# An iterated entmax stage: result matmuls taken apart by head, Newton steps spread one by one, three of eight relu pairs on ScalarE

## The chip, the cores and the metric

The kernel runs on one core of one Trainium2 chip. The metric is the time of one execution in microseconds (us), as the median of several runs on the chip: 2030.03 us for the kernel before (three runs, 2029.74 to 2032.66). Five engines work side by side and meet at semaphores: PE (TensorE, matrix products), DVE (VectorE), ACT (ScalarE), POOL (GpSimd) and SP (which issues DMAs). Each runs its own list of instructions strictly in order, so an instruction that waits holds up everything behind it on its engine.

## The reference, cut to what matters

The whole program is two residual blocks on x of 2 x 1024 x 256. The change touches one stage of the second block, a Hopfield layer (`_L1_attn_ref`): eight heads, a memory of 256 patterns, three steps of entmax with exponent 1.5, and an output projection.

```python
def entmax15(x):
    x = (x - jnp.max(x, -1, keepdims=True)) / 2.0
    ...
    return jnp.square(jnp.clip(x - tau_star, 0.0, None))
Q = layernorm(hidden, g_state, b_state) @ Wq.T
K, V = ...                               # of the normed memory, by head
xi = Q.reshape(B, S, H, hd).transpose(0, 2, 1, 3)
for _ in range(NUM_STEPS):               # 3
    scores = jnp.einsum('bhsd,hnd->bhsn', xi, K) * beta
    w = entmax15(scores)
    xi = jnp.einsum('bhsn,hnd->bhsd', w, V)
out = xi.transpose(0, 2, 1, 3).reshape(B, S, H * hd) @ Wo.T
```

tau_star is the threshold at which the squares of the clipped values sum to one. The kernel doesn't sort: it starts from a bound out of the eight largest scores and corrects the threshold in three rounds of a Newton-like step that needs the mean and the variance of the clipped scores.

## The kernel before, in words

The rows of x are 16 tiles of 128 rows. Two tiles make a chain; four chains make a group, and there are two groups. A work item g (0 to 23) is one of the three steps of one chain: items 0 to 3 are the first steps of group one, 4 to 7 their second steps, 8 to 11 their last, and 12 to 23 the same for group two. An item holds 16 score matrices (2 tiles x 8 heads) of 128 x 256, in the tile `sw[g % 5]`; two heads of one tile are a pair `q`, so an item has eight pairs.

The stage is a pipeline of 28 beats, written out by hand for each engine. In beat b:

- PE multiplies item b's scores in four quarters (`scores`, L1412, into `pss`), and turns (transposes) the squared weights of item b-3 pair by pair (`turn`, L1397, into the ring of two tiles `pt`). Where an item ends its chain (`ends`), its result is multiplied with the folded output weights (`result`, L1424, into `pz`); where a new chain begins, its normed rows are transposed (`state`, L1436, also into `pz`).
- ACT copies scores out (`sw<-pss`, L1488), makes the clipped scores of the first BY_ACT pairs of each round (`relus`, `ra`, L1468), takes the square roots (`root`, L1475), and for item b-3 cuts each pair with the final threshold (`cut`, L1495) and squares what PE has turned (`square`, `sw<-pt`, L1480). The order is cut 0, cut 1, cut 2, square 0, cut 3, square 1 and so on, with the last quarter of the scores and the root of round 1 in the middle.
- POOL makes the clipped scores of the other pairs (`most`, `rp`, L1569) behind two small instructions on `tau` and `step`, and weighs the sums of the largest (`spread`, L1577 and L1580).
- DVE finds the eight largest of each row (`largest`, L1725, 16 in a beat) and their running sums (L1599), the first threshold (`least`, L1606), the mean and variance of each clipped pair (`moments`: BATCH_NORM_STATS2, L1711 for ACT's pairs and L1715 for POOL's; 24 in a beat), and the Newton steps on 128 x 16 tiles (`newton`, L1623 to L1691). It also adds results to x (L1740) and writes the new states (`xt`, L1733).

Three items are in their rounds at once: in beat b item b-3 is in round 2, b-2 in round 1, b-1 in round 0. `newton` is a generator: each `yield` is a place where another instruction may come between two steps. `moments` calls `next` on it twice behind each of its eight instructions, and `finish` runs what is left. A round's threshold (`neg_made`) frees ACT's and POOL's clipped scores of the next round, and after round 2 ACT's cuts.

The rings that matter: `pss` and `pt` have two tiles each, `ra` seven and `rp` six, `pz` two, `sw` five items. Below, "turn phase" is the stretch of a beat in which PE's turns and ACT's cuts and squares follow each other, and "first turn" is its first turn on PE.

Of the kernel before, what the change touches and what calls it, by code (L numbers as in the profile page):

```python
# [16 lines left out]
P = 128  # L17
# [1298 lines left out]
class Hopfield(Stage):  # L1316
# [7 lines left out]
    BY_ACT = 4  # L1324
# [48 lines left out]

    def view(self, g, q):

        return self.sw[g % 5][:, q // 4, 2 * (q % 4):2 * (q % 4) + 2, :]
# [9 lines left out]
    def pe(self, e):  # L1386
# [40 lines left out]

        def state(g, i):
            n = self.tile(g, i)
            e.wait_ge(self.xn_made, n + 1)  # L1430
            if n >= 2:
                e.wait_ge(self.xt_made, n - 1)
            if self.ends(g - 6):
                e.wait_ge(self.y_out, self.tile(g - 6, i) + 1)
            for c in range(DC):
                x = e.transpose(self.pz[i][:, c * P:(c + 1) * P], self.xn[n % 2][:, c * P:(c + 1) * P], k.ident[:])  # L1436
            x.then_inc(self.state_in, 1)
# [3 lines left out]
        for beat in self.beats():  # L1441
            if beat < self.n:
                scores(beat, 0, 0)
                scores(beat, 0, 1)
            if self.begins(beat + 1):
                for i in range(2):
                    state(beat + 1, i)
            if beat < self.n:
                scores(beat, 1, 0)
                scores(beat, 1, 1)  # L1450
            for i in range(2):
                if self.ends(beat - 4):
                    result(beat - 4, i)
                if 0 <= beat - 3 < self.n:
                    for q in range(4 * i, 4 * i + 4):
                        turn(beat - 3, q)

    def act(self, e):
# [40 lines left out]
        for beat in self.beats():  # L1499
# [21 lines left out]
            if 2 in rounds:  # L1521
                root(rounds[2], 2)
# [85 lines left out]
    def newton(self, e, g, r, step, read_a, read_p):  # L1608
# [23 lines left out]
        if r == 0:  # L1632
            x.then_inc(self.asked[c], 1)
            step(e.reciprocal(rec, m))
            at = step.n
            yield
            e.wait_ge(self.root_made[c], 3 * (g // 4) + 1)
            step(e.tensor_tensor(root, z, root, ALU.subtract))
            yield
            e.wait_ge(self.math, step.n)  # L1640
# [52 lines left out]
    def dve(self, e):  # L1693
# [11 lines left out]
        def moments(g, r, between):  # L1705
            st = self.st[g % 4][r % 2]
            pool, act = range(self.BY_ACT, self.PAIRS), range(self.BY_ACT)
            for q in [*pool, *act] if r == 2 else [*act, *pool]:
# [9 lines left out]
                next(between, None)  # L1718
            finish(between)

        def largest(g, i, half):
            n = 4 * g + 2 * i + half
            e.wait_ge(self.s_made, n + 1)
            for h in range(4 * half, 4 * half + 4):
                e.max(self.top[g % 4][:, 8 * i + h, :], self.sw[g % 5][:, i, h, :]).then_inc(self.top_made, 1)  # L1725

        def state(g, i):
            n = self.tile(g, i)
            e.wait_ge(self.state_in, n + 1)
            if g >= 12:  # L1730
                e.wait_ge(self.scored, 4 * (g - 11))
            for c in range(DC):
                x = e.tensor_scalar(self.xt[g % 4][:, i, c, :], self.pz[i][:, c * P:(c + 1) * P], self.gs[:, c:c + 1],  # L1733
                                    self.bs[:, c:c + 1], ALU.mult, ALU.add)
            x.then_inc(self.xt_made, 1)
# [9 lines left out]
        for beat in self.beats():  # L1745
# [4 lines left out]
            finish(late)  # L1750
            if 1 <= beat <= self.n:
                self.least(e, beat - 1)
            if self.ends(beat - 5):
                result(beat - 5, 1)
            if w is not None:
                largest(w, 0, 0)
            after = self.newton(e, rounds[2], 2, step, self.bn_a, self.bn_p) if 2 in rounds else iter(())
            if 1 in rounds:
                moments(rounds[1], 1, after)
            finish(after)  # L1760
            if self.begins(beat + 1):
                for i in range(2):
                    state(beat + 1, i)
            if w is not None:
                largest(w, 0, 1)
            after = self.newton(e, rounds[1], 1, step, self.bn_a, self.bn_p) if 1 in rounds else iter(())
# [3 lines left out]
            if self.ends(beat - 4):  # L1770
                result(beat - 4, 0)
            late = self.newton(e, rounds[0], 0, step, self.bn_a, self.bn_p) if 0 in rounds else iter(())
            if w is not None:
                largest(w, 1, 0)
                largest(w, 1, 1)
# [793 lines left out]
```

## Time and profile before

| | us |
| --- | --- |
| median of three runs | 2030.03 |
| the profiled execution, its own time | 2029.85 |
| its span in the trace | 2028.1 |
| the Hopfield stage within it, first state to last addition | 718 to 1477 |
| mean granted TensorE clock | 0.905 of full |

| engine | busy us | share of the span |
| --- | --- | --- |
| PE | 1749.9 | 86% |
| DVE | 1545.7 | 76% |
| ACT | 1279.2 | 63% |
| POOL | 595.4 | 29% |

The shares are means over stages with different limits. In the profile's forty slices (50.7 us each) the Hopfield stage is slices 15 to 29. In most of them DVE stands at 99% and in four or five PE does; that is what has to be read by stretches. "Granted clock" is the share of its full 2.4 GHz that TensorE had in a stretch: 1.0 is all at 2.4 GHz, 0.5 all at 1.2.

### The profile page before, as it was taken

The numbers are of one execution on the slowest core, as the hardware profiler recorded it, in microseconds if no ns is written. First come the engines' busy times: TensorE is split into PE (matmuls) and PEld (weight loads), VectorE is DVE, ScalarE is ACT, GpSimd is POOL, SyncE is SP. The second block draws the span as 40 slices with busy tenths as digits, with TensorE's granted clock in tenths as the row PEclk, the third lists the DMA queues.
The fourth block names the chain that finished last, engine by engine and source line by source line (L and its number), as shares of the span: only waits on it lengthen the run. The fifth ranks groups of instructions, "written<-read, shape, count | busy, mean of one in ns | idle before, by whom it ended". The sixth has DMA issues, their size and how long they took to land. (4 is left out here: it accounts for less than half of the span.)

```text
span 2028.1 us, 32210 instructions
## 1 busy us (share of the span) xinstructions
PE 1749.9 (86%) x10498; PEld 1211.6 (60%) x10498; DVE 1545.7 (76%) x3465; ACT 1279.2 (63%) x2904; POOL 595.4 (29%) x1150
## 2 busy tenths in 40 slices
PE   4989799999998987888798988886867799998998
PEld 3558444444443775666677766665646355546787
DVE  6765889999993669999987699998266688826554
ACT  2543387777876437999875799997433288865111
POOL 2003122222222045445453344554034022224200
PEclk9989699999998987878999988888878599997999
DMA  3463132333310100000000000000025433110001
GB/s 115 134 198 63 32 64 64 64 64 65 64 33 14 58 1 1 1 0 1 1 1 1 1 1 1 1 1 1 1 75 141 89 64 64 33 56 15 1 1 42
DMA packets 36134, 82.54 MB, mean 41 GB/s; under 512 B 9600, under 2 KB 11776, under 8 KB 34944
## 3 DMA queue, kind: packets, MB, share of 16 engines
q1 hardware_dynamic: 35968, 80.48, 16.0%
q8 instruction: 85, 1.39, 0.3%
q14 instruction: 81, 0.66, 0.1%
HBM read 52.79 MB, written 27.26 MB: 39 GB/s over the span
## 5 line engine op out<-in xcount | busy, mean ns | idle before, releaser
L1035 ACT ACTIVATE probs<-pss 128x512 f32<-128x512 f32 (+3 forms) x1152 | 482.0, 496 | 132.7 <-PE pss L998 131.4
L1063 DVE TENSOR_REDUCE negmax<-px 128x2 f32<-128x1024 f32 (+2 forms) x480 | 506.7, 1113 | 51.8 <-PE px L979 48.4
L998 PE MATMUL pss<-queries,keys 64*128 64x512 f32 (+3 forms) x1152 | 296.8, 396 | 9.2 <-ACT probs L1035 5.6
L1569 POOL TENSOR_SCALAR rp<-sw,tau 128x256 f32<-128x256 f32 x576 | 274.0, 503 | 64.5 <-DVE st L1715 57.4
L979 PE MATMUL px<-keys,queries 63*128 63x512 f32 (+3 forms) x1152 | 270.1, 428 | 13.8 <-DVE negmax L1063 13.7
L1112 POOL TENSOR_SCALAR_AFFINE_SELECT probs<-probs 128x512 f32<-128x512 f32 x192 | 120.4, 635 | 532.4 <-ACT probs L1035 532.4
L998 PEld LDWEIGHTS pss<-queries,keys 64*128 64x128 f32 x1152 | 168.1, 190 | 155.8 <-ACT probs L1035 136.2
L1397 PE MATMUL pt<-ident,sw 128*128 128x128 f32 x768 | 155.6, 342 | 115.0 <-ACT sw L1480 75.3
L1012 PE MATMUL po<-probs,vals 128*32 128x512 f32 (+3 forms) x2304 | 247.3, 505 | 0.4 <-POOL probs L1112 0.2
L1468 ACT ACTIVATE ra<-sw,neg 128x256 f32<-128x256 f32 x576 | 243.3, 515 | 1.6 <-DVE neg L1691 1.6
L1412 PE MATMUL pss<-again,sw 128*128 128x256 f32 x1024 | 242.6, 401 | 0.0
L1412 PEld LDWEIGHTS pss<-again,sw 128*128 128x128 f32 x1024 | 208.1, 205 | 31.1
L1397 PEld LDWEIGHTS pt<-ident,sw 128*128 128x128 f32 x768 | 105.2, 172 | 165.4 <-ACT sw L1495 158.1
L1715 DVE BATCH_NORM_STATS2 st<-rp 128x6 f32<-128x512 f32 x288 | 194.0, 675 | 3.0 <-POOL rp L1569 3.0
L1711 DVE BATCH_NORM_STATS2 st<-ra 128x6 f32<-128x512 f32 x288 | 189.5, 679 | 7.1 <-ACT ra L1468 6.6
L1495 ACT ACTIVATE sw<-sw,neg 128x256 f32<-128x256 f32 x384 | 167.7, 497 | 19.6 <-DVE neg L1691 19.6
L979 PEld LDWEIGHTS px<-keys,queries 63*128 63x128 f32 x1152 | 132.6, 202 | 71.0 <-DVE negmax L1063 69.0
L1480 ACT ACTIVATE sw<-pt 128x512 f32<-128x512 f32 x192 | 111.1, 583 | 72.0 <-PE pt L1397 72.0
L1725 DVE MAX8 top<-sw 128x8 f32<-128x256 f32 x384 | 131.8, 410 | 10.5 <-ACT sw L1488 10.5
L1412 PE MATMUL pss<-vals,xt 128*128 128x256 f32 x512 | 119.0, 394 | 8.3 <-ACT sw L1488 8.3
L1424 PE MATMUL pz<-to_out,sw 128*128 128x256 f32 x512 | 118.4, 391 | 5.0 <-issue 4.1
L1488 ACT ACTIVATE sw<-pss 128x1024 f32<-128x1024 f32 x96 | 96.9, 1010 | 37.4 <-PE pss L1412 37.2
(355 smaller groups left out, 2591.8 us busy)
## 6 DMA issues: line engine op xcount, KB each, us to landing
queries<-rec_q SPq DMA_DIRECT2D x96, 128.0 KB, 3.5
keys<-rec_k SPq DMA_DIRECT2D x96, 128.0 KB, 3.6
queries<-rec_q SPq DMA_DIRECT2D x96, 64.0 KB, 3.4
keys<-rec_k SPq DMA_DIRECT2D x96, 64.0 KB, 3.5
rec_q<-fs SPq DMA_DIRECT2D x16, 256.0 KB, 4.4
rec_k<-fs SPq DMA_DIRECT2D x16, 256.0 KB, 4.6
rec_q<-vals SPq DMA_DIRECT2D x16, 256.0 KB
rec_k<-vals SPq DMA_DIRECT2D x16, 256.0 KB
```

Source lines behind the costliest of these rows:

```text
L979: x = e.matmul(px[:, n, s * width:(s + 1) * width], ops.qs[p][at:at + STACK, tile, t * P:(t + 1) * P], ops.ks[p][at:at + STACK, tile, c:c ...
L998: e.matmul(tl.pss[scores % 3][:, 512 - width:512], ops.ks[p][at:at + STACK + 1, tile, j * P:(j + 1) * P], ops.qs[p][at:at + STACK + 1, til ...
L1012: x = e.matmul(tl.po[32 * n:32 * n + 32, 512 - width:512], self.vals[:, u // H * QT + j, u % H, :], tl.probs[arg][:, n, :], start=j == 0, ...
L1035: e.activation(tl.probs[arg][:, w, :], tl.pss[scores % 3][:, 512 - width:512], ACT.Exp).then_inc(self.exp_made, 1)
L1063: e.tensor_reduce(out, from_px, X_AXIS, ALU.max, negate=True).then_inc(self.x_read, 1)
L1397: x = e.transpose(self.pt[n % 2][:, 2 * h + c, :], self.view(g, q)[:, h, c * P:(c + 1) * P], k.ident[:])
L1412: x = e.matmul(self.pss[n % 2][:, h, :], lhsT, rhs[:, 4 * half + h, c, :], start=c == 0, stop=c == 1)
L1468: x = e.activation(self.ra[n % 7][:, :, h], self.view(g, q)[:, h, :], ACT.Relu, bias=self.neg[c][:, 2 * q + h:2 * q + h + 1])
L1495: x = e.activation(self.view(g, q)[:, h, :], self.view(g, q)[:, h, :], ACT.Relu, bias=self.neg[c][:, 2 * q + h:2 * q + h + 1])
L1569: x = e.tensor_scalar(self.rp[rp % 6][:, :, h], self.view(g, q)[:, h, :], -BIG, self.tau[c][:, 2 * q + h:2 * q + h + 1], ALU.min, ALU.max)
L1711: e.bn_stats(st[:, q, :], self.ra[self.bn_a % 7][:].rearrange("p n h -> p (n h)")).then_inc(self.ra_read, 1)
L1715: e.bn_stats(st[:, q, :], self.rp[self.bn_p % 6][:].rearrange("p n h -> p (n h)")).then_inc(self.rp_read, 1)
```

## The change

Five edits, all in the class `Hopfield`.

1. `result` is one head instead of eight: two matmuls, with a wait for the square of that head's pair. A table `RESULTS` says per beat how many heads come before the second half of the scores, and how many behind each turn. Table `ADDS_EARLY` and `ADDS_LATE` place DVE's additions.
2. `state` transposes into `pt` instead of `pz`; the first two turns of such a beat wait until DVE has read it.
3. `BY_ACT` is 3 instead of 4: POOL makes five of eight pairs in each round.
4. Newton steps come one behind each BATCH_NORM_STATS2 (two where the pipeline runs empty), and one behind each maximum. Round 0 has eight empty places between its reciprocal and the step that waits for the root.
5. ACT takes the root of round 2 behind the second relu pair of round 0 instead of behind the last.

```diff
-    BY_ACT = 4
+    BY_ACT = 3
+    RESULTS = (((0, 0, 0) + (1,) * 8, (4,) + (1,) * 8, (4,) + (1,) * 8, (4,) + (1,) * 8, (4,) + (1,) * 8, (8,)),
+               ((0,), (16,), (16,), (16, 0, 0) + (2,) * 8))
+    ADDS_EARLY = {12: [(8, 0)], 13: [(8, 1)], 14: [(9, 0), (9, 1)], 15: [(10, 0)], 16: [(10, 1), (11, 0)], 25: [(20, 1)],
+                  26: [(21, 1)]}
+    ADDS_LATE = {16: [(11, 1)], 24: [(20, 0)], 25: [(21, 0)], 26: [(22, 0), (22, 1)], 27: [(23, 0)]}
...
 # turn(g, q)
+            if q < 2 and self.begins(g + 4):
+                e.wait_ge(self.xt_made, self.tile(g + 4, q) + 1)
...
-        def result(g, i):
+        def result(g, i, h):
             n = self.tile(g, i)
-            state = max(m for m in range(min(g + 6, self.n)) if self.begins(m))
-            e.wait_ge(self.wt_made, 8 * g + 4 * i + 4)
-            e.wait_ge(self.xt_made, self.tile(state, i) + 1)
-            if n >= 2:
+            e.wait_ge(self.wt_made, 8 * g + 4 * i + h // 2 + 1)
+            if h == 0 and n >= 2:
                 e.wait_ge(self.y_out, n - 1)
-            for h in range(HH):
-                for c in range(2):
-                    x = e.matmul(self.pz[i][:], self.turned_view(g, i, h, c), k.to_out[:, h, c, :],
-                                 start=(h, c) == (0, 0), stop=(h, c) == (HH - 1, 1))
-            x.then_inc(self.y_in, 1)
+            for c in range(2):
+                x = e.matmul(self.pz[i][:], self.turned_view(g, i, h, c), k.to_out[:, h, c, :],
+                             start=(h, c) == (0, 0), stop=(h, c) == (HH - 1, 1))
+            if h == HH - 1:
+                x.then_inc(self.y_in, 1)
...
 # PE, for each beat
+            before, among = self.results(beat)
...
+            for part in before:
+                result(*part)
             if beat < self.n:
                 scores(beat, 1, 0)
                 scores(beat, 1, 1)
-            for i in range(2):
-                if self.ends(beat - 4):
-                    result(beat - 4, i)
-                if 0 <= beat - 3 < self.n:
-                    for q in range(4 * i, 4 * i + 4):
-                        turn(beat - 3, q)
+            for q in range(self.PAIRS + 2):
+                if q < self.PAIRS and 0 <= beat - 3 < self.n:
+                    turn(beat - 3, q)
+                for part in among[q]:
+                    result(*part)
...
 # newton, round 0
             x.then_inc(self.asked[c], 1)
+            yield
             step(e.reciprocal(rec, m))
+            for _ in range(8):
+                yield
+            e.wait_ge(self.root_made[c], 3 * (g // 4) + 1)
+            step(e.tensor_tensor(root, z, root, ALU.subtract))
...
 # moments
                 next(between, None)
-                next(between, None)
-            finish(between)
+                if g + r + 1 >= self.n:
+                    next(between, None)
...
+        def largest(g, i, half, between):
...
                 e.max(self.top[g % 4][:, 8 * i + h, :], self.sw[g % 5][:, i, h, :]).then_inc(self.top_made, 1)
+                next(between, None)
```

Where it moves instructions. First PE in beat 13, a beat with results and a new state. `vals` is the score matrix of first steps, `x16` counts matmuls; L1412 is the scores, L1436 the state, L1424 the results, L1397 the turns (four transposes to a pair). Before:

```order
L1412 MATMUL pss<-vals,xt 128x256 x16
L1436 MATMUL pz<-ident,xn 128x128 x4
L1412 MATMUL pss<-vals,xt 128x256 x16
L1424 MATMUL pz<-to_out,sw 128x256 x16
L1397 MATMUL pt<-ident,sw 128x128 x16
L1424 MATMUL pz<-to_out,sw 128x256 x16
L1397 MATMUL pt<-ident,sw 128x128 x16
```

Now the same beat, with L1433 for the scores, L1455 the state, L1442 the results and L1418 the turns; its last two rows come six times more:

```order
L1433 MATMUL pss<-vals,xt 128x256 x16
L1455 MATMUL pt<-ident,xn 128x128 x4
L1442 MATMUL pz<-to_out,sw 128x256 x8
L1433 MATMUL pss<-vals,xt 128x256 x16
L1418 MATMUL pt<-ident,sw 128x128 x4
L1442 MATMUL pz<-to_out,sw 128x256 x2
L1418 MATMUL pt<-ident,sw 128x128 x4
L1442 MATMUL pz<-to_out,sw 128x256 x2
```

Sixteen heads in two blocks, one of them between turns 3 and 4, became four heads in a block and one behind each turn.

Second, PE at the end of the stage, from beat 25 on. Before, the last 32 matmuls are both results of item 23:

```order
L1424 MATMUL pz<-to_out,sw 128x256 x16
L1397 MATMUL pt<-ident,sw 128x128 x16
L1424 MATMUL pz<-to_out,sw 128x256 x16
L1397 MATMUL pt<-ident,sw 128x128 x16
L1424 MATMUL pz<-to_out,sw 128x256 x16
L1397 MATMUL pt<-ident,sw 128x128 x16
L1424 MATMUL pz<-to_out,sw 128x256 x16
L1397 MATMUL pt<-ident,sw 128x128 x16
L1424 MATMUL pz<-to_out,sw 128x256 x32
```

Now, from item 22's turns (the first row), with item 22's results behind them and item 23's heads two behind each turn from the third:

```order
L1418 MATMUL pt<-ident,sw 128x128 x32
L1442 MATMUL pz<-to_out,sw 128x256 x32
L1418 MATMUL pt<-ident,sw 128x128 x12
L1442 MATMUL pz<-to_out,sw 128x256 x4
L1418 MATMUL pt<-ident,sw 128x128 x4
L1442 MATMUL pz<-to_out,sw 128x256 x4
L1418 MATMUL pt<-ident,sw 128x128 x4
L1442 MATMUL pz<-to_out,sw 128x256 x4
```

No turn is preceded by half an item's results any more, and what follows the last turn is six heads (twelve matmuls) instead of sixteen.

Third, DVE behind the first threshold in an ordinary beat: the Newton steps of round 2 (L1623 to L1660 here). Before:

```order
L1725 MAX top<-sw 128x8 x4
L1711 BN_STATS st<-ra 128x6
L1623 TENSOR_TENSOR st<-st,neg 128x8
L1627 TENSOR_TENSOR m_356<-st 128x16
L1711 BN_STATS st<-ra 128x6
L1631 SCALAR_TENSOR_TENSOR z<-m_356,st 128x16
L1645 SCALAR_TENSOR_TENSOR w<-st 128x16
L1647 RECIPROCAL inv<-step 128x16
L1651 TENSOR_TENSOR y<-z 128x16
L1711 BN_STATS st<-ra 128x6
L1656 TENSOR_TENSOR y<-y,inv 128x16
L1660 SCALAR_TENSOR_TENSOR y<-w,y 128x16
```

Now (L1748 is the maximum, L1644, L1648, L1652 and on the same Newton steps, L1734 the statistics of ACT's pairs):

```order
L1748 MAX top<-sw 128x8
L1644 TENSOR_TENSOR st<-st,neg 128x10
L1748 MAX top<-sw 128x8
L1648 TENSOR_TENSOR m_356<-st 128x16
L1748 MAX top<-sw 128x8
L1652 SCALAR_TENSOR_TENSOR z<-m_356,st 128x16
L1668 SCALAR_TENSOR_TENSOR w<-st 128x16
L1670 RECIPROCAL inv<-step 128x16
L1748 MAX top<-sw 128x8
L1674 TENSOR_TENSOR y<-z 128x16
L1734 BN_STATS st<-ra 128x6
L1679 TENSOR_TENSOR y<-y,inv 128x16
```

Each small step stands alone behind a large instruction; the last two of a round, on `step` and `neg`, still follow each other, now behind all eight statistics instead of seven.

## Rows read from the trace of the kernel before

**Rows 1.** Busy time by stretch: an ordinary beat, beats 11 to 16, seven ordinary beats.

```profile
core 0: us, PE busy (x) PEld busy (x) DVE busy (x) ACT busy (x) POOL busy (x), PEclk, DMA share, GB/s
914.80:941.60 26.80, 21.42 (x96) 17.22 (x96) 26.16 (x82) 24.33 (x56) 13.29 (x32) 0.87 0.00 1
1005.30:1179.20 173.90, 153.15 (x748) 130.05 (x748) 137.89 (x430) 122.46 (x276) 74.09 (x161) 0.97 0.00 1
1196.30:1384.00 187.70, 152.64 (x674) 122.47 (x673) 183.11 (x568) 171.36 (x388) 93.19 (x218) 0.85 0.00 1
```

**Rows 2.** Timeline of PE, beats 11 and 12: start, us, what [idle before].

```profile
1005.35 1.46 PE L1397 MATMUL pt<-ident,sw 128*128 128x128 f32 x8 [0.37 <-ACT sw L1495]
...
1025.85 7.07 PE L1412 MATMUL pss<-vals,xt 128*128 128x256 f32 x32
...
1043.45 0.63 PE L1397 MATMUL pt<-ident,sw 128*128 128x128 f32 x4 [0.65 <-ACT sw L1480]
1043.91 7.07 PE L1424 MATMUL pz<-to_out,sw 128*128 128x256 f32 x32
```

**Rows 3.** Timeline of PE, end of beat 16.

```profile
1179.21 0.66 PE L1397 MATMUL pt<-ident,sw 128*128 128x128 f32 x4 [2.26 <-ACT sw L1495]
```

**Rows 4.** DVE's waits, 1005 to 1170: who waited for whom, total, times, longest.

```profile
DVE rec L1679 <- ACT root L1475: 19.7, 4, 6.6
```

**Rows 5.** Timeline of DVE in the ordinary beat from 914.84.

```profile
914.84 0.27 DVE L1606 TENSOR_REDUCE neg<-sums 128x16 f32<-128x128 f32 x1
...
917.29 0.45 DVE L1627 TENSOR_TENSOR m<-st 128x16 f32<-128x16 f32 x1
917.66 0.69 DVE L1711 BATCH_NORM_STATS2 st<-ra 128x6 f32<-128x512 f32 x1
918.26 0.42 DVE L1631 SCALAR_TENSOR_TENSOR z<-m,st 128x16 f32<-128x16 f32 x1
...
923.37 0.17 DVE L1691 SCALAR_TENSOR_TENSOR neg<-step,neg 128x16 f32<-128x16 f32 x1
...
927.81 0.16 DVE L1656 TENSOR_TENSOR y<-y,inv 128x16 f32<-128x16 f32 x1
928.00 0.18 DVE L1660 SCALAR_TENSOR_TENSOR y<-w,y 128x16 f32<-128x16 f32 x1
928.09 0.69 DVE L1711 BATCH_NORM_STATS2 st<-ra 128x6 f32<-128x512 f32 x1
...
938.57 0.17 DVE L1691 SCALAR_TENSOR_TENSOR neg<-step,neg 128x16 f32<-128x16 f32 x1
```

**Rows 6.** Timeline of POOL in the same beat.

```profile
916.76 1.92 POOL L1569 TENSOR_SCALAR rp<-sw,tau 128x256 f32<-128x256 f32 x4
921.43 1.89 POOL L1569 TENSOR_SCALAR rp<-sw,tau 128x256 f32<-128x256 f32 x4 [2.76 <-DVE st L1715]
...
939.42 3.78 POOL L1569 TENSOR_SCALAR rp<-sw,tau 128x256 f32<-128x256 f32 x8
```

**Rows 7.** Timeline of ACT in the same beat: first cuts, relus of round 2, first score copy.

```profile
923.58 2.50 ACT L1495 ACTIVATE sw<-sw,neg 128x256 f32<-128x256 f32 x6 [0.78 <-DVE neg L1691]
...
935.79 1.72 ACT L1468 ACTIVATE ra<-sw,neg 128x256 f32<-128x256 f32 x4
...
940.15 1.02 ACT L1488 ACTIVATE sw<-pss 128x1024 f32<-128x1024 f32 x1 [0.86 <-PE pss L1412]
```

**Rows 8.** Timeline of PE at the end of the stage.

```profile
1392.71 1.97 PE L1397 MATMUL pt<-ident,sw 128*128 128x128 f32 x8 [7.79 <-ACT sw L1495]
...
1397.04 7.93 PE L1424 MATMUL pz<-to_out,sw 128*128 128x256 f32 x32
...
1447.43 1.46 PE L1397 MATMUL pt<-ident,sw 128*128 128x128 f32 x8 [2.25 <-ACT sw L1495]
...
1462.59 13.98 PE L1424 MATMUL pz<-to_out,sw 128*128 128x256 f32 x64
```

**Rows 9.** Timeline of DVE, last addition of the stage.

```profile
1476.60 0.42 DVE L1740 TENSOR_TENSOR x<-x,pz 128x256 f32<-128x256 f32 x1 [6.49 <-PE pz L1424]
```

More of the change, by code:

```diff
@@ L1372, in beats, with results @@
         return range(self.n + self.CHAINS)
+    def results(self, beat):
+        before, among = [], [[] for _ in range(self.PAIRS + 2)]
+        for last, table in zip((self.n // 2, self.n), self.RESULTS):
+            first = last - self.CHAINS
+            todo = [(g, i, h) for g in range(first, last) for i in range(2) for h in range(HH)]
+            if 0 <= beat - first - 3 < len(table):
+                at = sum(map(sum, table[:beat - first - 3]))
+                counts = table[beat - first - 3]
+                before, at = todo[at:at + counts[0]], at + counts[0]
+                for q, count in enumerate(counts[1:]):
+                    among[q], at = todo[at:at + count], at + count
+        return before, among
     def view(self, g, q):
@@ L1432, in state @@
                 e.wait_ge(self.xt_made, n - 1)
-            if self.ends(g - 6):
-                e.wait_ge(self.y_out, self.tile(g - 6, i) + 1)
+            if g >= 4:
+                e.wait_ge(self.wt_made, 8 * (g - 4))
             for c in range(DC):
-                x = e.transpose(self.pz[i][:, c * P:(c + 1) * P], self.xn[n % 2][:, c * P:(c + 1) * P], k.ident[:])
+                x = e.transpose(self.pt[i][:, c, :], self.xn[n % 2][:, c * P:(c + 1) * P], k.ident[:])
             x.then_inc(self.state_in, 1)
@@ L1520, in act @@
                     ra += 1
-            if 2 in rounds:
-                root(rounds[2], 2)
+                if q == 1 and 2 in rounds:
+                    root(rounds[2], 2)
             if w is not None:
@@ L1633, in newton @@
             x.then_inc(self.asked[c], 1)
+            yield
             step(e.reciprocal(rec, m))
+            for _ in range(8):
+                yield
+            e.wait_ge(self.root_made[c], 3 * (g // 4) + 1)
+            step(e.tensor_tensor(root, z, root, ALU.subtract))
             at = step.n
             yield
[L1637 to L1640, printed above, removed]
+            e.wait_ge(self.math, at)
             step(e.tensor_tensor(move, root, rec, ALU.mult))
@@ L1717, in moments @@
                 next(between, None)
-                next(between, None)
-            finish(between)
-        def largest(g, i, half):
+                if g + r + 1 >= self.n:
+                    next(between, None)
+        def largest(g, i, half, between):
             n = 4 * g + 2 * i + half
@@ L1750, in dve @@
             finish(late)
+            after = self.newton(e, rounds[2], 2, step, self.bn_a, self.bn_p) if 2 in rounds else iter(())
             if 1 <= beat <= self.n:
                 self.least(e, beat - 1)
-            if self.ends(beat - 5):
-                result(beat - 5, 1)
+            for tile in self.ADDS_EARLY.get(beat, ()):
+                result(*tile)
             if w is not None:
-                largest(w, 0, 0)
-            after = self.newton(e, rounds[2], 2, step, self.bn_a, self.bn_p) if 2 in rounds else iter(())
+                largest(w, 0, 0, after)
             if 1 in rounds:
@@ L1760, in dve @@
             finish(after)
+            after = self.newton(e, rounds[1], 1, step, self.bn_a, self.bn_p) if 1 in rounds else iter(())
             if self.begins(beat + 1):
@@ L1764, in dve @@
             if w is not None:
-                largest(w, 0, 1)
-            after = self.newton(e, rounds[1], 1, step, self.bn_a, self.bn_p) if 1 in rounds else iter(())
+                largest(w, 0, 1, after)
             if 0 in rounds:
@@ L1769, in dve @@
             finish(after)
-            if self.ends(beat - 4):
-                result(beat - 4, 0)
+            for tile in self.ADDS_LATE.get(beat, ()):
+                result(*tile)
             late = self.newton(e, rounds[0], 0, step, self.bn_a, self.bn_p) if 0 in rounds else iter(())
             if w is not None:
-                largest(w, 1, 0)
-                largest(w, 1, 1)
+                largest(w, 1, 0, late)
+                largest(w, 1, 1, late)
                 self.start(e, w)
```

2 lines of the change are left out of this document (1 added, 1 removed).

## The prediction

> **What bounds the kernel now.** First the table of stretches [rows 1]: it shows two different limits inside one stage. In an ordinary beat of 26.8 us DVE is busy 26.16; seven such beats in a row take 187.7 us, 26.8 each, and there are fifteen (beats 4 to 10 and 16 to 23). In beats 11 to 16, where results are multiplied, PE has 748 matmuls in 173.9 us instead of 96 in 26.8, its clock is 0.97 of full (2.4 GHz nearly throughout), and DVE falls to 138 busy of 174. So the fifteen ordinary beats are DVE's, and about five are PE's. Second, PE's timeline in the latter [rows 2, 3]: from item 8's first turn at 1005.35 to item 13's at 1179.21 the reader sees 32 records (16 matmuls) go by in 7.07 us, in a block ahead of turn 0 and one between turns 3 and 4. ACT can't square what isn't turned, so its queue stands, and with it the roots behind it: DVE waited 19.7 us for one kind of them [rows 4]. Third, DVE's timeline in an ordinary beat [rows 5] against POOL's [rows 6] and ACT's [rows 7]; fourth, the end of the stage [rows 8, 9], where two whole results of item 23 (13.98 us) come behind its last turn. The next stage starts behind the last addition at 1477.0, so what the stage gains the program gains.
>
> **Beats 11 to 16 (edit 1).** A head is two matmuls: 7.07 / 8 = 0.88 us. A turn costs PE 0.46 where it needs no wait (1043.45 to 1043.91) [rows 2]. ACT's pace is a cut pair and a square, about 1.28 us: from the first cut at 923.58 to the first relu behind the last square at 935.79 are 12.2 us, with one score copy of 1.0 inside [rows 7]. So PE has 1.28 - 0.46 = 0.82 us free per turn today, and one head of 0.88 fits nearly whole. Turn phase with eight heads: 8 x (0.46 + 0.88) = 10.7 us, PE never idle. Of one beat: scores 2 x 7.07 = 14.1, four heads 3.5, state (four transposes, as a turn) 0.46, turn phase 10.7: 28.8 us. From first turn to first turn:
> - item 8 to 9: phase 11.0 (heads lag two turns) + 14.1 + 3.5 + 0.46 = 29.1
> - 9 to 10 and 10 to 11: 28.8 each
> - 11 to 12 (no state): 28.4
> - 12 to 13 (eight heads in a block ahead of the scores' second half): 10.7 + 14.1 + 7.1 = 31.9
>
> Together 147.0 against 173.9 [rows 2, 3]. The matmuls are the same; what goes is the time in which PE had nothing to do but turns. What is late next is DVE: its own beat (26.9 below) plus four state instructions (1.3) and one or two additions (0.3 each) is 28.5 to 28.8, level with PE. Two queues level with each other cost something; I take 0.5 us in each of five beats: 149.5, a gain of 24.4. The bounds: 26.9 (PE alone) and, if DVE's beat is 1.5 us longer than I think, 17.
>
> **State into pt (edit 2).** Removes the wait of results for DVE's reading of `pz`; adds one of turns 0 and 1 for the same reading. Behind that waiting turn stands all of PE. DVE writes the state right behind round 2's threshold, about 1.3 us after it; PE reaches the first turn some 3 us later still in a PE-bound beat (scores' start + 18.1, against + 15.7). Nothing there; at worst 1 us in four beats.
>
> **The end (edit 1).** Before, from item 21's first turn at 1392.71 to 1477.0: 84.3 us [rows 8, 9]. Now in PE's order: item 21's turns, undisturbed, 12.2 - 1.0 - 0.9 (first cut) = 10.3; item 21's results 14.0, plus 1.0 since the turns leave the clock low (the block at 1397.04 took 7.93 for 7.07); item 22's turns 9.0 (cuts ready); its results 14.2; item 23: three turns 1.4, five times two heads and a turn 5 x 2.23 = 11.2, six heads 5.3, addition 0.4. Sum 66.8, a gain of 17.5. It needs thresholds in time: item 22's turns come at + 25.3, item 23's at + 48.5, against + 54.7 before (1447.43). The blocks of results between turns, which held back ACT's squares and with them the roots [rows 4], stood here too, and in the new order there are none; I work item 22's threshold out at about + 22 and item 23's at + 41, so PE stays the later one. I take 16, bounds 10 (threshold of item 23 late by six) and 18.
>
> **Ordinary beats: what Newton steps win (edits 4, 5).** Two small steps in a row cost 0.19 for the first (927.81 to 928.00), alone 0.09 (928.00 to 928.09) [rows 5]: 0.10 is the wait of the second for the first. Fourteen such pairs stand in a beat (six in each of rounds 2 and 1, two in round 0); two remain. That is 12 x 0.10 = 1.2 us, and about 0.2 for round 0's step that waited for its root. ACT's six relus less save nothing: it waits 0.78 for the threshold before its cuts and 0.86 for PE before a score copy [rows 7].
>
> **What they lose (edits 3, 4).** L1627 took 0.45 and L1631 0.42 while POOL was at work (916.76 to 918.68); the like instructions took 0.18 in POOL's idle time, and each ended with a POOL instruction [rows 5, 6]. Such a step behind a statistic then costs 0.24 more (two POOL instructions, 0.93 us, instead of 0.60 + 0.09), behind a maximum 0.05 once in step (one POOL instruction of 0.47 instead of 0.33 + 0.09). Today that is some five steps and 1.05 us a beat: POOL's stretches happen to lie beside round 2's first steps and round 0's. Now POOL has ten instructions per round for eight, 4.8 us; round 1's begin about 0.9 us behind round 0's threshold (938.57 to 939.42 today) [rows 5, 6], which itself comes two statistics later, so they run until 4.3 us after the first threshold; then round 0's first pair, a pause of 0.7, and four pairs as fast as DVE frees the ring, until 10. All of round 2's Newton steps (0.5 to 9.8) lie in that. Going along: 0.5 in the maxima, 0.25 x 5 behind statistics, 0.2 at the end: 2.0. Round 1 is free; round 0 three steps in the maxima 0.3 and the root step behind `spread` 0.25. Sum 2.55, 1.5 more than today. DVE's beat: 26.8 - 1.4 + 1.5 = 26.9. Bounds of the extra: 0 and, with all 25 such steps of a beat behind statistics hit, 6.0 - 1.05 = 5.
>
> The Trainium skill ("SBUF — State Buffer", Who interferes with whom) says it as a rule: a DVE instruction with two inputs in SBUF and a GpSimd one that reads SBUF exclude each other for a whole instruction, and who begins first has it. The rows above agree for the loser DVE (0.45 for 0.18). By the rule BATCH_NORM_STATS2 and MAX8, with one input, are never held, so only small steps pay.
>
> A second circle closes round those beats. Threshold of round 2 (923.37), cuts, turns, PE's first quarter, its copy (ends 941.17) [rows 5, 7] is 17.8 us; then the maxima, and from them to the next threshold 8.35 us today (914.84 + 0.18 to 923.37), together 26.2, hidden by 0.6. In the new order the threshold is behind eight statistics instead of seven (+0.6), with its first steps in the maxima, and pays the 2.0: I get 9.4. 17.9 + 9.4 = 27.3. DVE's own beat gives 26.9; I take 27.1, so + 0.3 in fifteen beats, + 4.5. The first beats, where POOL fills an empty pipeline with five pairs instead of four: + 1.
>
> **Sum.** The profiled execution took 2029.85, its span 2028.1 (1.75 around it), 0.2 under the median of 2030.03. 2029.85 - 24.4 - 16 + 4.5 + 1 = 1995.0.
>
> **Rivals.**
> - *The steps win and POOL costs little.* For it: POOL's stretches today touch only five of 25 steps. Against: the same 0.24 each time they do. Then DVE's beat is 25.6, but the second circle stays at 26.0 or so: - 0.8 instead of + 0.3 in 15 beats, and beats 11 to 15 reach PE's 28.8: 1995 - 16.5 - 2 = 1976.5.
> - *DVE takes over beats 11 to 15, and the circle is dearer.* For it: 28.8 and 28.6 lie side by side, and POOL also makes the new states there (two instructions of 1.2 us, held against DVE's steps). 30.3 per beat instead of 29.3 in five, + 0.9 instead of + 0.3 in fifteen, end 13 instead of 16: 1995 + 5 + 9 + 3 = 2012.
> - *Interleaved heads hold up the turns* (the change doesn't do what it says): a head waits for its square in PE's queue, and each turn behind it waits too. In beats 12 to 15 its squares are a beat old; only beat 11 and item 23 mix an item's heads with its own turns, two turns behind. If ACT's 1.28 rules there instead of PE's 1.34 nothing is lost; if each head stalls by a square (0.5), 16 x 0.5 = + 8: 2003.
> - *Slower than before.* POOL's load is what decides: its work per beat goes from 13.3 to about 16.2 us [rows 1], and if its instructions slide along with DVE's steps through all three rounds, nearly every two-input step pays 0.24. 5.0 - 1.4 = + 3.6 per beat, x 15 = + 54, and + 2 in each of beats 11 to 15: 2029.85 - 40.4 + 54 + 10 + 1 = 2054. It decides from + 2.6 per ordinary beat (39 / 15). Against: the ring lets POOL run ahead no more than six pairs, so it must be idle some 10 us of each beat, and I find that idle time beside round 1.
>
> **Chances.** Forecast 0.52, first rival 0.17, second 0.20, third 0.06, slower 0.05. From 1976.5 and 2012 and their own width: 1976 to 2013. 0.2% is 4 us, about what a measurement here tells from no change; between 2026 and 2034 lies only a slice of the second and the last case: 0.03. Slower 0.03, faster 0.94.
>
> **What would show it.** Right: beats 11 to 15 at 28.5 to 30 us from threshold to threshold and PE nearly without idle time in them; DVE's waits for roots there gone; from item 21's first turn to the last addition 66 to 70 us; ordinary beats 26.8 to 27.3; round 2's small steps mostly at 0.3 to 0.45, round 1's at 0.16 to 0.18. Wrong: ordinary beats of 26 or less (first rival) or 27.7 and more (second), round 1's steps long too (last), a PE idle before its turns in beats 11 to 15, or idle before item 22's or 23's turns at the end (thresholds late).

## The result, and the profile after

The changed kernel took 1987.2 us (median of four runs, 1985.87 to 1992.4), the one before beside it 2031.35 (2029.74 to 2035.56). The ratio is 0.9782, 95% interval 0.9768 to 0.9797. The forecast was 1995.0 with a range of 1976 to 2013. The profiled execution took 1986.14 (span 1984.4) against 2029.85: 43.7 us less, which the two traces place so:

| stretch | before | after | difference | forecast |
| --- | --- | --- | --- | --- |
| up to item 8's first turn | 1005.35 | 1007.09 | + 1.7 | ordinary beats and start, + 5.5 in all |
| item 8's to item 13's first turn | 173.9 | 146.3 | - 27.6 | - 24.4 |
| item 13's to item 21's first turn | 213.5 | 214.5 | + 1.0 | (with the first line) |
| item 21's first turn to the last addition's end | 84.3 | 66.3 | - 18.0 | - 16 |
| the stages behind | 551.1 | 550.2 | - 0.9 | 0 |

The changed kernel's own repeats differ by as much outside the stage (550.2 and 552.2 us behind it in two of them), so only the second and the fourth line are clear gains.

First the table of stretches of the changed kernel, with the columns of [rows 1]: an early ordinary beat, a late one, item 8's to item 13's first turn, and the end.

```profile
833.60:859.60 26.00, 21.63 (x94) 17.15 (x93) 25.48 (x82) 21.34 (x49) 16.17 (x38) 0.80 0.00 1
...
940.80:968.10 27.30, 21.89 (x98) 17.60 (x97) 26.41 (x83) 22.18 (x50) 16.19 (x39) 0.87 0.00 1
1007.10:1153.40 146.30, 143.85 (x749) 126.07 (x750) 141.30 (x448) 112.54 (x249) 88.77 (x191) 1.00 0.00 1
1367.80:1434.20 66.40, 58.97 (x288) 49.28 (x288) 34.68 (x111) 39.15 (x93) 15.23 (x36) 0.92 0.00 1
```

In the middle PE is busy 143.85 of 146.3, its clock full, and DVE 141.3: both at once, where before PE had 153 of 174 and DVE 138 [rows 1]. So of the 27.6 us, 18.3 are idle time of PE (20.75 before, 2.45 now) and 9.3 are busy time for the same matmuls. The second part the prediction didn't have. Some of it shows in the rows: a turn that stands alone is a record of 0.63 us [rows 2], in a row with heads the next instruction starts 0.44 behind it; and one block before ran partly at the low clock (8.83 us for 7.07, shown at e2). Now the timeline of PE there (L1418 turns, L1442 results, L1433 scores, L1455 state): item 8's first turn and the longest wait among its turns, then a piece of beat 12.

```profile
1007.09 1.46 PE L1418 MATMUL pt<-ident,sw 128*128 128x128 f32 x8 [1.11 <-ACT sw L1516]
...
1014.95 0.63 PE L1418 MATMUL pt<-ident,sw 128*128 128x128 f32 x4 [1.59 <-ACT sw L1501]
...
1038.32 0.60 PE L1418 MATMUL pt<-ident,sw 128*128 128x128 f32 x4
1038.75 1.03 PE L1442 MATMUL pz<-to_out,sw 128*128 128x256 f32 x4
1039.62 0.60 PE L1418 MATMUL pt<-ident,sw 128*128 128x128 f32 x4
1040.06 1.03 PE L1442 MATMUL pz<-to_out,sw 128*128 128x256 f32 x4
...
1048.74 7.07 PE L1433 MATMUL pss<-vals,xt 128*128 128x256 f32 x32
```

A turn and a head take 1.30 us (1038.32 to 1039.62), none of beat 12's rows has a wait in brackets, and a beat is 28.12 (first turn to first turn, 1038.32 to 1066.44). All the waiting of this stretch, 2.3 us, is inside item 8's turns. The counterpart is [rows 2]. DVE had waited there for two kinds of roots, the one of [rows 4] and, in the same answer, that of round 0 (first line, before). Of the second nothing is left, of the first (second line, 1005 to 1154):

```profile
DVE root L1638 <- ACT root L1475: 13.6, 4, 3.5
...
DVE rec L1702 <- ACT root L1496: 2.9, 4, 1.5
```

One wait of 4.3 us for such a root follows right behind, at 1158, in item 13's turns.

The end of the stage on PE and DVE, against [rows 8, 9]; `x64` is sixteen heads:

```profile
1367.85 1.45 PE L1418 MATMUL pt<-ident,sw 128*128 128x128 f32 x8 [0.27 <-ACT sw L1516]
...
1377.39 14.75 PE L1442 MATMUL pz<-to_out,sw 128*128 128x256 f32 x64
1391.98 1.04 PE L1418 MATMUL pt<-ident,sw 128*128 128x128 f32 x8
...
1400.97 14.90 PE L1442 MATMUL pz<-to_out,sw 128*128 128x256 f32 x64
1415.71 1.04 PE L1418 MATMUL pt<-ident,sw 128*128 128x128 f32 x8
```

```profile
1433.77 0.42 DVE L1764 TENSOR_TENSOR x<-x,pz 128x256 f32<-128x256 f32 x1 [7.37 <-PE pz L1442]
```

Items 22 and 23 start turning at + 24.1 and + 47.9 behind item 21's first turn (forecast + 25.3 and + 48.5), with no wait in brackets: PE, not a threshold, sets them.

The ordinary beats are hardly gain or loss (- 0.1 and + 2.4 us in the two sets of seven), but they changed inside. The first threshold came every 26.1 to 26.7 us at first in each half, then every 27.3. DVE's timeline of such a late beat (L1627 first threshold, L1748 maxima, L1714 the thresholds, L1734 and L1738 statistics), against [rows 5]:

```profile
940.82 0.26 DVE L1627 TENSOR_REDUCE neg<-sums 128x16 f32<-128x128 f32 x1
941.68 0.43 DVE L1748 MAX8 top<-sw 128x8 f32<-128x256 f32 x1 [0.60 <-ACT sw L1509]
...
943.68 0.48 DVE L1674 TENSOR_TENSOR y<-z 128x16 f32<-128x16 f32 x1
944.08 0.68 DVE L1734 BATCH_NORM_STATS2 st<-ra 128x6 f32<-128x512 f32 x1
944.69 0.40 DVE L1679 TENSOR_TENSOR y<-y,inv 128x16 f32<-128x16 f32 x1
...
948.52 0.33 DVE L1699 TENSOR_SCALAR y<-y 128x16 f32<-128x16 f32 x1
...
950.77 0.39 DVE L1714 SCALAR_TENSOR_TENSOR neg<-step,neg 128x16 f32<-128x16 f32 x1
...
953.54 0.15 DVE L1679 TENSOR_TENSOR y<-y,inv 128x16 f32<-128x16 f32 x1
```

POOL in the same beat (L1590 its clipped pairs), against [rows 6]; then ACT's first cuts and its first score copy, against [rows 7], with PE's last turn of the beat between them:

```profile
940.37 4.70 POOL L1590 TENSOR_SCALAR rp<-sw,tau 128x256 f32<-128x256 f32 x10
945.16 0.20 POOL L1580 TENSOR_SCALAR tau<-neg 128x16 f32<-128x16 f32 x1
945.46 0.96 POOL L1590 TENSOR_SCALAR rp<-sw,tau 128x256 f32<-128x256 f32 x2
947.34 3.81 POOL L1590 TENSOR_SCALAR rp<-sw,tau 128x256 f32<-128x256 f32 x8 [0.92 <-DVE st L1738]
```

```profile
951.20 2.50 ACT L1516 ACTIVATE sw<-sw,neg 128x256 f32<-128x256 f32 x6 [0.38 <-DVE neg L1714]
...
961.73 1.09 PE L1418 MATMUL pt<-ident,sw 128*128 128x128 f32 x4 [0.19 <-ACT sw L1501]
...
967.91 1.02 ACT L1509 ACTIVATE sw<-pss 128x1024 f32<-128x1024 f32 x1 [1.92 <-PE pss L1433]
```

The same step L1679 costs 0.40 where POOL runs (944.69) and 0.15 where it doesn't (953.54): POOL is busy to 951.15, over all of round 2's steps, with a pause from 946.42 to 947.34, as forecast. And DVE waits 0.60 for a score copy (941.68); the next one waits 1.92 for PE. PE is slow there: its last turn is a record of 1.09 us, where a turn at full clock is 0.60 to 0.63, and from the scores' start at 962.61 to the copy are 5.3 us. That is the circle: threshold 950.77 to copy's end 968.93 is 18.2 us, maxima 941.68 to threshold 950.77 is 9.1, together 27.3.

### The profile page after: what moved, and what is told of

It reads as the page before. It is cut to its first block and busy times, and to the rows that moved or that the text cites. A ratio compares the mean times of both kernels' runs of the same rounds, so it can differ in the third digit from the quotient of the medians.

```text
span 1984.4 us, 32136 instructions
## 1 busy us (share of the span) xinstructions
PE 1736.3 (87%) x10498; PEld 1204.1 (61%) x10498; DVE 1546.2 (78%) x3465; ACT 1224.2 (62%) x2760; POOL 664.9 (34%) x1294
## 5 line engine op out<-in xcount | busy, mean ns | idle before, releaser
L1590 POOL TENSOR_SCALAR rp<-sw,tau 128x256 f32<-128x256 f32 x720 | 343.5, 504 | 18.5 <-DVE st L1738 11.4
L1433 PE MATMUL pss<-again,sw 128*128 128x256 f32 x1024 | 243.0, 401 | 0.0
L1738 DVE BATCH_NORM_STATS2 st<-rp 128x6 f32<-128x512 f32 x360 | 238.2, 679 | 4.8 <-POOL rp L1590 4.7
L1418 PE MATMUL pt<-ident,sw 128*128 128x128 f32 x768 | 150.9, 331 | 92.8 <-ACT sw L1501 67.2
L1433 PEld LDWEIGHTS pss<-again,sw 128*128 128x128 f32 x1024 | 208.6, 206 | 31.0
L1489 ACT ACTIVATE ra<-sw,neg 128x256 f32<-128x256 f32 x432 | 187.9, 516 | 7.6 <-DVE neg L1714 7.0
L1418 PEld LDWEIGHTS pt<-ident,sw 128*128 128x128 f32 x768 | 103.7, 167 | 140.0 <-ACT sw L1516 134.3
L1748 DVE MAX8 top<-sw 128x8 f32<-128x256 f32 x384 | 147.9, 406 | 17.9 <-ACT sw L1509 17.9
L1734 DVE BATCH_NORM_STATS2 st<-ra 128x6 f32<-128x512 f32 x216 | 144.4, 680 | 0.1
L1501 ACT ACTIVATE sw<-pt 128x512 f32<-128x512 f32 x192 | 112.2, 589 | 27.1 <-PE pt L1418 27.1
L1433 PE MATMUL pss<-vals,xt 128*128 128x256 f32 x512 | 118.6, 392 | 5.7 <-ACT sw L1509 5.7
L1442 PE MATMUL pz<-to_out,sw 128*128 128x256 f32 x512 | 122.2, 387 | 0.0
```

The lines of the kernel that those rows point to most:

```text
L1433: x = e.matmul(self.pss[n % 2][:, h, :], lhsT, rhs[:, 4 * half + h, c, :], start=c == 0, stop=c == 1)
L1489: x = e.activation(self.ra[n % 7][:, :, h], self.view(g, q)[:, h, :], ACT.Relu, bias=self.neg[c][:, 2 * q + h:2 * q + h + 1])
L1590: x = e.tensor_scalar(self.rp[rp % 6][:, :, h], self.view(g, q)[:, h, :], -BIG, self.tau[c][:, 2 * q + h:2 * q + h + 1], ALU.min, ALU.max)
L1738: e.bn_stats(st[:, q, :], self.rp[self.bn_p % 6][:].rearrange("p n h -> p (n h)")).then_inc(self.rp_read, 1)
```

## The experiments

All ratios are to the kernel before, on the same chip. "Beat" is the common distance of first thresholds in ordinary beats, DVE L1606 or its counterpart. e6, e7, e9 and e10 ran on a chip on which the kernel before took 2037.27 us, against 2031.54 (e1, e2, e3, e5) and 2030.22 (e11, e12, e13) on the others. So ratios from different chips can differ by some 0.3% for that alone (e1 and e9 are alike beat by beat, and 0.9773 and 0.9748), and small differences are read from the beats.

**e1: results alone.** From the changed kernel:

```diff
-    BY_ACT = 3
+    BY_ACT = 4
 # newton, moments, largest, and ACT's root of round 2: as before
```

> Edits 1 and 2 alone (results by head, state in pt; four of eight pairs on ScalarE, Newton steps in twos, root of round 2 behind all relus, as before). My theory: the gain is the results' alone. From item 8's first turn to item 13's 147 to 150 us instead of 173.9, from item 21's first turn to the last addition 66 to 68 instead of 84.3, ordinary beats 26.8 as before: 2029.85 - 25 - 17 = 1988, within 5 of the changed kernel. Rival (the results gain only because the lighter ScalarE and the spread steps keep the roots in time): at least 8 us slower than the changed kernel, 1995 or more, with DVE waiting for roots in beats 12 to 15.

1987.69 us, ratio 0.9773 (0.9749 to 0.9798), beat 26.8; item 8's to item 13's first turn 147.0 us, item 21's to the last addition 67.6, both as expected. From the 11th to the 17th first threshold it took 173.1 us (changed kernel 173.3, before 200.9), from the last one to the last addition 76.3 (75.5, before 93.0). The whole gain is that of edits 1 and 2; the lighter ScalarE isn't needed for it. How it divides between the two no run tells: edit 2 alone was not run. Its new wait shows here once, 1.7 us ahead of item 8's first turns:

```profile
1004.60 1.27 PE L1418 MATMUL pt<-ident,sw 128*128 128x128 f32 x8 [1.69 <-DVE xt L1754]
```

**e2: edits 3 to 5 alone**, on the kernel before, whose `result` and `state` stay.

```diff
-    BY_ACT = 4
+    BY_ACT = 3
 # newton, moments, largest, root: as changed
```

> Edits 3 to 5 alone (three of eight pairs on ScalarE, Newton steps one at a time also behind maxima, root earlier), results in blocks of eight heads as before. My theory: what the steps win the port and the longer circle take back: ordinary beats start at 26.1 to 26.4 and settle at 27.3, beats 12 to 15 unchanged at 36 to 38: 2029.85 + 0 to + 4, so 2030 to 2034. Rival (the steps are a gain of their own of 1 us a beat): 2015 or less.

2024.26 us, ratio 0.9967 (0.9952 to 0.9982): 7 less than before, under my range, above the rival's. Ordinary beats were as expected: + 1.7 and + 0.7 us in the two sets of seven, beat 26.1 to 27.3. The miss is in beats 11 to 17: 194.8 instead of 200.9. There PE's wait at the result was 1.2 us instead of 2.03 (first line before, second e2). By the code it is the wait for DVE's reading of the state in `pz`; the profile finds no releaser for it ("issue").

```profile
1070.53 8.83 PE L1424 MATMUL pz<-to_out,sw 128*128 128x256 f32 x32 [2.03 <-issue]
...
1069.57 7.14 PE L1424 MATMUL pz<-to_out,sw 128*128 128x256 f32 x32 [1.19 <-issue]
```

The block itself took 7.14 instead of 8.83. Together with the same wait a beat later (2.05 before, 1.22 now) these rows hold 3.4 of the 6 us; the rest I didn't take apart. With the results spread, wait and slow block are gone anyway.

**e3: the changed kernel with four pairs on ScalarE.**

```diff
-    BY_ACT = 3
+    BY_ACT = 4
```

> The changed kernel with BY_ACT = 4: POOL has 12 instead of 15 pairs in a beat, all else as changed. My theory: fewer of round 2's Newton steps meet a POOL instruction (about 1.5 us a beat instead of 2.0), but two more relu pairs and a copy stand behind the early root, 2.7 us where 2.2 are hidden, so cuts start up to 0.5 later: the circle keeps its 27.3, 1984 to 1990, no difference from the changed kernel beyond 4 us. Rival A (POOL's load is what costs the ordinary beats): their beats fall to 26.5, 1977 or less. Rival B (a lighter ScalarE is worth something): 1993 or more.

1987.4 us, ratio 0.9774 (0.9752 to 0.9797), beat 25.9 at first and then 27.2. No difference, as the theory had it: as long as the circle sets the beat, POOL's load doesn't show.

**e5: matmuls that nobody reads, in ordinary beats' turn phases.**

```diff
+        def warm(beat, count):
+            if beat in (*range(3, 11), *range(17, 24)):
+                if beat > 16:
+                    e.wait_ge(self.y_out, 7)
+                for _ in range(count):
+                    e.matmul(self.pz[0][:], k.ident[:], k.to_out[:, 0, 0, :], start=True, stop=True)
...
                     turn(beat - 3, q)
+                    warm(beat, (1, 1, 1, 3, 1, 1, 1, 0)[q])
```

> The changed kernel with one matmul of 128x256 that nobody reads behind each of the first seven turns of an ordinary beat (three behind the fourth), into pz, which is free then. It adds no result and no reader. Theory (the ordinary beats at 27.3 are a circle through PE at half clock after the turns): granted clock near 1.0 there, the first quarter of the scores 3.5 instead of about 5 us, DVE no longer waits for the first score copy, beats at DVE's own 26.3 to 26.5: 9 to 12 us less than the changed kernel, 1975 to 1978. Rival (the clock plays no part, or the added matmuls hold the turns up by as much): 1986 or more.

1974.86 us, ratio 0.9722 (0.9699 to 0.9745), just under my range, and 12.5 us under e3 (1987.4) on the same chip. The beat was 25.95 to 26.0, in the first and the last three of the second half 26.3 to 27.3. Busy time and clock of two beats, with the columns of [rows 1]:

```profile
911.00:937.00 26.00, 22.41 (x116) 18.23 (x115) 25.71 (x83) 22.07 (x51) 16.34 (x38) 1.00 0.00 1
937.00:963.00 26.00, 23.64 (x116) 19.69 (x115) 25.68 (x82) 22.12 (x51) 16.31 (x38) 0.93 0.00 1
```

More matmuls on PE, and the kernel is 12 us faster: the granted clock is 0.93 to 1.00 instead of 0.80 to 0.87. PE's last turn is a record of 0.63 instead of 1.09, the scores' start (931.52) to the first copy takes 3.66 us instead of 5.3, and the copy hardly waits:

```profile
931.05 0.63 PE L1418 MATMUL pt<-ident,sw 128*128 128x128 f32 x4 [0.22 <-ACT sw L1510]
...
935.18 1.02 ACT L1518 ACTIVATE sw<-pss 128x1024 f32<-128x1024 f32 x1 [0.32 <-PE pss L1433]
```

DVE waits for nothing in these beats. So the circle through PE at low clock was what bound the changed kernel's ordinary beats, and 26.0 is DVE's own work.

**e9: results alone, with the same matmuls** (e1 with e5's edit).

> Edits 1 and 2 alone (four of eight pairs on ScalarE, Newton steps in twos) with the added matmuls in ordinary beats. Theory (with the steps in twos VectorE's own 26.8 bounds the beats, and the circle has slack): nothing gained over edits 1 and 2 alone, 1984 to 1989, though the granted clock rises; so the changed kernel's steps are worth 10 us or more only together with the added matmuls. Rival (a warmer TensorE helps any version): 1978 or less.

1987.31 us, ratio 0.9748 (0.9734 to 0.9762) against 0.9773 of e1 on another chip; beat 26.8, as without, and the two sets of seven beats are equal to e1's within 0.7 us. The clock of ordinary beats rose from 0.81 to 0.87 to mostly 0.94 to 1.00 and nothing came of it: with steps in twos DVE's own 26.8 hides the circle.

**e6: e5 with four pairs on ScalarE** (`BY_ACT = 4`).

> The kernel with the added matmuls (one that nobody reads behind each turn of an ordinary beat), and BY_ACT = 4: POOL makes four of eight pairs. The ordinary beats are now VectorE's own work (26.0 us, no wait), so the price of the shared port shows. Theory (POOL's two more instructions per round cost some 0.4 us a beat by meeting Newton steps): beats of 25.5 to 25.7, 1968 to 1972. Rival (the port is the same either way, POOL's instructions only move): 25.9 to 26.1, 1973 to 1977. Second rival (two more relu pairs behind the early root hold the cuts up): 26.4 and more, above 1979.

1968.76 us, ratio 0.9671 (0.9654 to 0.9689) against 0.9722 of e5, part of it the chip; beat 25.6 to 25.7 in most. The ordinary beats give about 4 us, the end 2 (74.3 for 76.3 from the last first threshold). More is in it than shows, for DVE waited for ACT's roots (five beats):

```profile
DVE rec L1711 <- ACT root L1505: 4.2, 5, 0.9
```

Without that 0.84 a beat it would be 24.8, an estimate. My second rival was right that two more relu pairs hold something up (the root, not the cuts), and wrong in the size.

**e11: e5 with two pairs on ScalarE** (`BY_ACT = 2`, POOL 18 pairs a beat).

> The kernel with the added matmuls and BY_ACT = 2: POOL makes six of eight pairs, 18 in a beat, after 12 (25.65 us a beat) and 15 (25.97). Theory (each of POOL's instructions costs VectorE's Newton steps some waiting): another 0.3 to 0.6 us, beats of 26.3 to 26.6, 0.3% to 0.5% over the kernel with 15 pairs. Rival (the difference between 12 and 15 pairs was something else): 26.0.

1982.7 us, ratio 0.9760 (0.9743 to 0.9777), 0.4% over e5; but the beat was 26.16, only 0.2 more, under my range. Most of the 8 us is at the edges: ahead of the stage's first threshold (1.4 us later), the pipeline's filling (from the first to the third 1.4 more), the beats next to the middle, and the end (77.6 for 76.3).

**e13: e5 with steps in twos, three pairs on ScalarE.**

```diff
                 next(between, None)
-                if g + r + 1 >= self.n:
-                    next(between, None)
+                next(between, None)
+            finish(between)
 # none behind maxima; root of round 2 behind all relus
```

> The added matmuls, three of eight pairs on ScalarE, but Newton steps in twos and none behind maxima, root of round 2 behind all relus. Of the square of steps (twos or single) and pairs on ScalarE (four or three), in twos with four gave 26.8 a beat, single with four 25.65, single with three 25.97. Theory (both effects add: twos cost 1.1, POOL's load 0.3): 27.1, so 12 to 17 us more than the kernel with the added matmuls and single steps. Rival (in twos the steps miss POOL's instructions, so its load is free): 26.8.

2003.05 us, ratio 0.9862 (0.9846 to 0.9879), beat 27.45: 28 us over e5, where I had expected 12 to 17. Where the circle doesn't bind, the beats form a square (e9, e13, e6, e5):

| beat, us | four pairs on ScalarE | three |
| --- | --- | --- |
| steps in twos | 26.8 | 27.45 |
| steps one at a time | 25.65 (0.84 of it waiting for a root) | 25.97 |

Single steps are worth 1.1 to 1.5 us a beat; the third pair given to POOL costs 0.65 in twos and 1.1 singly, of which ACT's late root hides 0.8.

**e7: round 2's steps in twos behind statistics.**

```diff
-                if g + r + 1 >= self.n:
+                if g + r + 1 >= self.n or r == 1:
```

> The changed kernel, but the Newton steps of round 2 again two behind each statistic (those behind maxima stay single). Its threshold comes three statistics earlier, about 1.8 us, and VectorE's own beat is 0.3 to 0.4 longer by steps that follow each other. Theory (ordinary beats are a circle from that threshold over cuts, turns and the first quarter of the scores back to the maxima): beats fall from 27.3 to VectorE's own 26.3 to 26.5, 1975 to 1980. Rival (the beats are 27.3 for another reason, as the clock's rhythm itself): 27.3 as before or more, 1986 and up.

1987.83 us, ratio 0.9756 (0.9741 to 0.9771); beat 26.3 or 27.1: my theory's 1975 to 1980 was missed. Round 2's threshold did come earlier (8.2 us behind the first threshold, 943.88 to 952.10, instead of 9.95), and ACT and PE show where that went:

```profile
952.56 2.50 ACT L1516 ACTIVATE sw<-sw,neg 128x256 f32<-128x256 f32 x6 [0.19 <-DVE neg L1714]
...
960.26 0.22 ACT L1496 ACTIVATE root<-y 128x16 f32<-128x16 f32 x1 [1.25 <-DVE y L1699]
```

```profile
961.90 1.09 PE L1418 MATMUL pt<-ident,sw 128*128 128x128 f32 x4 [2.56 <-ACT sw L1501]
```

In the middle of the cuts stands round 1's root, and that is asked for by DVE at a time of its own. Cuts that start earlier stand 1.25 us before it. So the circle has a second spoke; I had left it out. That it is this wait which kept the beats long is read from one beat, no run took it away.

**e10: e5 with such matmuls also in beats 24 and 25**, into `pss`.

> The kernel with the added matmuls, with such matmuls also behind the turns of beats 24 and 25 (into pss, free by then), ahead of the result blocks. Theory: the two blocks of 32 matmuls take 14.0 each instead of 14.8 and 14.6, 1 to 2 us less, 1973 to 1974, hardly to be told from 1974.9. Rival (the end waits for thresholds, which they hold up): 1977 or more.

1975.02 us, ratio 0.9692 (0.9678 to 0.9705). The end took 73.9 us instead of 76.3, somewhat more than expected; in the time of a run that can't be told from e5's.

**e12: all of it** (e10 with `BY_ACT = 4`), and the changed kernel again on the same chip.

> The added matmuls in ordinary beats and in beats 24 and 25, with BY_ACT = 4: all that helped together. Beats of 25.7, the end from the last first threshold to the last addition 73 instead of 75.5: about 20 us (1.0%) under the changed kernel. Rival (a gain at one place is given back at the other): within 14 us of it.

> The changed kernel again, on the same chip as the others of this set, to compare with directly: ratio to the kernel before 0.977 to 0.980, ordinary beats 26.1 at first and 27.3 later.

1965.13 us, ratio 0.9678 (0.9665 to 0.9692); the changed kernel 1987.32, ratio 0.9781 (0.9766 to 0.9796). 22 us less side by side (20 expected), with beats of 25.5 to 25.6 and an end of 73.1: the best version of this study, with nothing computed less. The changed kernel's beats were again 26.0 to 26.3 at times and 27.3 late in each half, as expected.

## Why the prediction was right, point by point

- **Beats 11 to 16.** The mechanism was right: PE works through the beats with hardly an idle moment. Mis-sized was PE's own sum. Of the 146.3 us measured PE waited 2.3, so PE alone is 144.0, where I had 147.0. Four beats without a wait took 28.1, 28.1, 27.7 and 31.1 for my 28.8, 28.8, 28.4 and 31.9: I had added up records (7.07 for sixteen matmuls, 0.46 + 0.88 for a turn and a head), but the next block starts 6.9 behind, the next turn 1.30. The 2.5 us that I added for two queues level with each other came out in size (2.3), by luck: they are not spread over five beats but all in item 8's turns, which follow ACT's squares (31.2 for my 29.1).
- **State in pt.** The new wait costs nothing, as forecast: no wait of turn 0 or 1 for it in beats 11 to 14 (in e1 one of 1.7 us, once). What the edit takes away I had put at no figure: before, results waited 0.9, 2.0 and 2.05 us for the state in three beats, 5.0 of the 20.75 idle.
- **The end.** 66.8 worked out, 16 taken instead of 17.5 for doubt about thresholds; 66.3 and 18.0 measured. The doubt was the error.
- **Ordinary beats.** Forecast 26.9 for DVE's own work and 27.3 for the circle, 27.1 taken. Measured 27.3 where the circle binds (18.2 and 9.1, forecast 17.9 and 9.4, two small errors that cancel; the 9.4 stood there without its sum), and 26.9 and 27.2 over the two sets of seven, since each half begins with beats of 26.1 to 26.7 before PE is late. DVE's own work is 25.97 (e5): this term was 0.9 too dear. The step that failed is the port's price, 2.55 us a beat. By the same sum (26.8 - 1.4 + c - 1.05 = 25.97) it is 1.6. The steps at 946.49 and 947.17 fell into POOL's pause where I had reckoned with one, and that at 947.85 took 0.15 beside a working POOL. A saved pair is worth 0.115 (0.19 less 0.075), not 0.10, which would make the port's price 1.8. It cost the total little, as the circle lay above.
- **Rivals.** The first (steps win, POOL costs little) was half there: DVE's own 26.0 would have shown, but the circle took it back, and e5 lets it out. The second had the circle's place but too high a price. The slower one needed + 2.6 a beat; even 18 pairs on POOL gave 26.2. The third (heads hold up the turns) didn't come: no head waited, in the middle or at the end; only turns did, for ACT, 0.7 and 1.6 us in item 8.
- **The signs.** From threshold to threshold beats 11 to 15 took 27.7 to 29.5, a little under the 28.5 to 30 named. Of round 2's small steps only six of some fourteen took 0.3 or more in the beat shown, not most; round 1's were at 0.14 to 0.18, as named.
- The 8.9 us between 1995.0 and 1986.1 are: middle 3.2 (3.0 of it PE's sum), end 2.0, ordinary beats and start 2.8, the stages behind 0.9 (no more than repeats differ).

## What to carry to other kernels

Where an engine is paced by another in one stretch and works alone in the next, take the second stretch's work apart and put it into the first one's gaps, small enough to fit (here 0.88 us into 0.82): the gain is close to the whole of it, and worked out from two rows. A saving on the engine that is busy 98% may be given back by a circle that lay just below it; measure each circle's length in the trace before, and look for a second wait inside it. Here spread work also kept TensorE's clock up (1.00 for 0.97 in beats 11 to 16, and e5), and in e5 that was worth more than the added work cost. It was worth nothing where DVE was the bound (e9).

## What the runs showed of the hardware

- Matmuls that nobody reads made the kernel 0.6% faster (e5 against e3). With TensorE idle between turns the granted clock of an ordinary beat was 0.80 to 0.88 of full, with the gaps filled 0.93 to 1.00, and the first quarter of the scores ran at 2.4 GHz: 3.66 us up to its copy instead of 5.3.
- In the prediction I took from the rule on two inputs that only small steps pay. BATCH_NORM_STATS2 (0.63 to 0.70 with POOL running or not) and MAX8 (0.36 to 0.43) were indeed never held, nor was RECIPROCAL (0.22 to 0.26). But TENSOR_SCALAR on 128x16 (L1699) took 0.33 at 948.52, with POOL running, and 0.15 where POOL stood. The Trainium skill ("SBUF — State Buffer", Who interferes with whom) lists `tensor_scalar` among the operations that can enter a mode with two ports and so contend with GpSimd; the trace agrees (0.33 for 0.15), and I had read only the line on two inputs.
- The price depends on rhythm, not on load alone. Steps of over 0.27 us, counted over ten ordinary beats, number per beat 4.1 before, 7.0 in the changed kernel (6.1 in its repeat), 6.0 in e5, 7.0 in e11 with 18 pairs, but 1.5 in e6 with 12. That is not because POOL is idle beside them in e6: in the beat from 908.47 it works from 908.03 to 916.33 with short pauses, over all but the last two of round 2's steps. One of these takes 0.40, two take 0.25, the others begin near the end of a POOL instruction or between two and pay nothing:

```profile
908.03 3.87 POOL L1599 TENSOR_SCALAR rp<-sw,tau 128x256 f32<-128x256 f32 x8
...
912.29 1.90 POOL L1599 TENSOR_SCALAR rp<-sw,tau 128x256 f32<-128x256 f32 x4
...
912.62 0.18 DVE L1696 SCALAR_TENSOR_TENSOR y<-z,y 128x16 f32<-128x16 f32 x1
...
913.33 0.40 DVE L1700 TENSOR_TENSOR y<-y,inv 128x16 f32<-128x16 f32 x1
```

What sets this rhythm no run tells.
